# First key stores issued sooner, batch 3's statistics sooner, and turn eight's product order

## The reference

```python
x = x + tanh(g_xattn[0]) * L0_xattn(layernorm(x), ctx, ctx)      # 16 heads, causal
x = x + tanh(g_ffn[0])   * L0_ffn(layernorm(x), w_gate_up, w_proj)   # ternary weights by groups of 64
x = x + tanh(g_xattn[1]) * L1_xattn(layernorm(x), ctx, q_w, ..., o_w)  # q, k normed; softmax over 256 keys
x = x + tanh(g_ffn[1])   * L1_ffn(layernorm(x), w_norm, w_gv, w_out)
# L1_ffn: h = rmsnorm(x) * w_norm; value, gate = quant(h) @ quant(w_gv); u = value * silu(gate)
#         x + quant(u) @ quant(w_out), with 8-bit integers for activations and ternary weights
```

## Time and profile before

| | |
|---|---|
| runs | 1144.2, 1140.21, 1139.71 us, median 1140.21 |
| profiled execution | 1139.14 us, span 1137.4 us |
| PE busy | 1096.0 us of the span |
| DVE, ACT, POOL busy | 832.7, 567.2, 74.5 us |
| mean granted clock of PE | 0.994 |
| transfers | 79.24 MB, most in the first third |

### The profile page before, as it was taken

One profiled execution on the slowest core, in us unless ns is written; L12 is line 12 of the kernel. 1 busy time (PEld: TensorE's weight loads), 2 busy tenths in 40 slices (PEclk: granted clock), 3 DMA queues, 4 the chain that ended last, 5 costly groups with the idle time before them and its releaser, 6 DMA issues.

```text
span 1137.4 us, 25529 instructions
## 1 busy us (share of the span) xinstructions
PE 1096.0 (96%) x10342; PEld 669.3 (59%) x10450; DVE 832.7 (73%) x1440; ACT 567.2 (50%) x918; POOL 74.5 (7%) x180
## 2 busy tenths in 40 slices
PE   8899999999999999999999999899999999999998
PEld 3455555556777777777777655455454545454543
DVE  5688888788767648566565667886868778777795
ACT  3676667766433333333333452455554637372654
POOL 0000000000000000000001012010101010101010
PEclk9899999999999999999999999999999999999999
DMA  9565555443212011021010201101010100000001
GB/s 361 185 194 169 181 193 156 154 122 122 67 38 65 20 38 37 20 75 28 29 57 20 84 2 38 37 2 56 1 57 1 57 1 30 10 11 11 10 10 38
DMA packets 29268, 79.24 MB, mean 70 GB/s; under 512 B 3041, under 2 KB 3297, under 8 KB 28897
## 3 DMA queue, kind: packets, MB, share of 16 engines
q1 hardware_dynamic: 29152, 77.61, 21.0%
HBM read 65.02 MB, written 12.58 MB: 68 GB/s over the span
## 4 chain that ended last, share of the span: by engine, by line
PE 89%; issue 3%; ACT 3%; DVE 2%; DMA 2%; SPq 1%; POOL 0%; ACTq 0%; DVEq 0%; POOLq 0%
PE bank L587 10%; PE bank L586 10%; PE bank L692 10%; PE bank L672 9%; PE bank L545 9%; PE bank L795 8%; PE bank L425 5%; PE bank L825 5%; PE bank L783 5%; PE bank L745 3%; PE bank L764 3%; PE bank L477 2%; PE bank L498 2%; PE bank L510 2%; PE bank L450 2%
## 5 line engine op out<-in xcount | busy, mean ns | idle before, releaser
L586 PE MATMUL bank<-ARENA,W 128*128 128x256 f16 x1024 | 227.3, 273 | 0.7 <-issue 0.7
L587 PE MATMUL bank<-ARENA,W 128*128 128x256 f16 x1024 | 227.2, 273 | 0.0
L1002 ACT ACTIVATE ARENA<-bank 128x512 f32<-128x512 f32 (+3 forms) x143 | 92.9, 687 | 81.3 <-PE bank L425 32.6
L545 PE MATMUL bank<-ARENA 128*128 128x512 f32 x256 | 119.4, 609 | 1.4 <-DMA ARENA<-in_wkv 1.4
L795 PE MATMUL bank<-W,ARENA 128*128 128x512 bf16 x493 | 116.6, 382 | 2.5 <-issue 0.7
L692 PE MATMUL bank<-ARENA 128*128 128x512 f32 x256 | 116.9, 600 | 0.0
L672 PE MATMUL bank<-W,ARENA 128*128 128x512 bf16 x472 | 114.6, 379 | 2.2 <-issue 0.2
L586 PEld LDWEIGHTS bank<-ARENA,W 128*128 128x128 bf16 x1024 | 100.0, 98 | 19.5 <-issue 1.3
L587 PEld LDWEIGHTS bank<-ARENA,W 128*128 128x128 bf16 x1024 | 100.1, 98 | 17.9
L1002 ACT ACTIVATE ARENA<-ARENA 128x512 f16<-128x512 f32 x64 | 40.3, 630 | 136.1 <-DVE ARENA L1585 129.6
L1585 DVE SCALAR_TENSOR_TENSOR ARENA<-bank,ARENA 128x512 f32<-128x512 f32 x64 | 48.0, 750 | 76.4 <-PE bank L587 73.5
(11 more groups left out here) (179 smaller groups left out, 1766.5 us busy)
## 6 DMA issues: line engine op xcount, KB each, us to landing
W<-in_w SPq DMA_DIRECT2D x48, 512.0 KB, 4.0
ARENA<-in_w SPq DMA_DIRECT2D x24, 512.0 KB, 3.6
kv_store<-ARENA SPq DMA_DIRECT2D x32, 256.0 KB, 3.8
W<-kv_store SPq DMA_DIRECT2D x15, 512.0 KB, 4.0
ARENA<-in_ctxT SPq DMA_DIRECT2D x8, 512.0 KB, 3.8
X<-in_x SPq DMA_DIRECT2D x8, 512.0 KB, 5.8
ARENA<-in_ctx SPq DMA_DIRECT2D x8, 512.0 KB, 5.9
out<-X SPq DMA_DIRECT2D x16, 256.0 KB, 2.0
```

Source lines behind the costliest of these rows:

```text
L545: mm = pe.matmul(bank, bufA["KT"][:, b % 2 * KD + k, t * P:(t + 1) * P], W[:, k, :], start=(k == 0), stop=(k == KD - 1 and what == 1))
L586: pe.matmul(bank[:, i * S:(i + 1) * S], W0[:, at:at + P], xt_half(b, 0)[:, k, :], start=(k == 0), stop=False)
L587: mm = pe.matmul(bank[:, i * S:(i + 1) * S], W0[:, at:at + P], xt_half(b, 1)[:, k, :], start=False, stop=(k == KD - 1))
L1002: return act.activation(to, src, ACT.Copy)
```

## The change

On SP the first store of keys is issued behind the constants and ahead of `load_w0(1)`, the second behind `load_values(0)` and ahead of `load_w0(2)`. On DVE, in turn 2, `stats(3)` goes ahead of `d_weighted(0)` and `c_norm_x(3)` ahead of the first `c_weigh`. In the eighth turn PE takes `d_turn_u(d, 0)` and `d_out_product(d, 0)` between the groups of the attention and `d_turn_u(d, 1)` ahead of the last `c_weigh`; ACT rounds both halves of the first tile between gates 5 and 6, and the second tile ahead of the last exponentials; DVE makes the first integers behind gate 6 and the second between `c_weigh` 1 and 2, and stores and takes the peak ahead of the last `c_weigh`. One bank is changed for it, that of `ut0.1`.

```diff
--- before.py
+++ after.py
@@ -261,7 +261,7 @@
         for turn in range(3, NB):
             places.turn(turn, ("g0 v1 g3 pq0 v6 v7 ut0.0 y0 xt0", "v0 po1 v3 g4 v5 g7 tq1 w1 w2 w3", "po0 g2 kt0 v4 pq1 w0 qt1 ut1.1 y1",
                                "g1 v2 kt1 g5 g6 mt tq0 ut0.1 qt0 ut1.0 xt1"))
-        places.turn(NB, ("g0 v1 g3 v5 v7 w1 w3", "v0 po1 v3 g6 g7 ut0.0 y0", "po0 g2 g4 g5 mt w0 ut0.1", "g1 v2 v4 v6 w2"))
+        places.turn(NB, ("g0 v1 g3 v5 v7 w1 w3", "v0 po1 v3 g6 g7 ut0.0 y0", "po0 g2 g4 g5 mt w0", "g1 v2 v4 v6 ut0.1 w2"))
         places.last.update({n: (s.c_ex, 8 * NB) for n in range(4)})
         a, b, c = NB - 3, NB - 2, NB - 1
         ends = ([("po0", c), ("ut1.0", a), ("ut1.1", a), ("po1", c), ("qt0", b), ("qt1", b), ("y1", a)]
@@ -344,8 +344,10 @@
             sp.dma_start(pre["masks"], masks).then_inc(s.ld_sel, 16)
             sp.dma_start(pre["selq"], selq).then_inc(s.ld_sel, 16)
             sp.dma_start(pre["selc"], selc).then_inc(s.ld_sel, 16)
+            store_kv(0, 0)
             load_w0(1)
             load_values(0)
+            store_kv(0, 1)
             load_w0(2)
             load_x(1)
             load_w1(0)
@@ -353,8 +355,6 @@
             load_w1(1)
             load_w0(3)
             load_w0(4)
-            store_kv(0, 0)
-            store_kv(0, 1)
             for turn in range(1, NB + 1):
                 f, b = turn, turn - 1
                 load_w0(3 * turn + 2)
@@ -962,15 +962,18 @@
             d_value_gate(d, 6)
             c_max_turn(b)
             d_value_gate(d, 7)
-            for g in range(NG):
-                c_probs(b, g)
-                if g:
-                    c_weigh(b, g - 1)
+            c_probs(b, 0)
+            c_probs(b, 1)
+            c_weigh(b, 0)
             d_turn_u(d, 0)
+            c_probs(b, 2)
+            c_weigh(b, 1)
+            d_out_product(d, 0)
+            c_probs(b, 3)
+            c_weigh(b, 2)
+            d_turn_u(d, 1)
             c_weigh(b, 3)
-            d_out_product(d, 0)
             c_project_out(b, 0)
-            d_turn_u(d, 1)
             c_project_out(b, 1)
             d_turn_q(c)
             d_out_product(d, 1)
@@ -1305,19 +1308,19 @@
             d_gate(d, 1)
             d_residual(d, 0)
             d_residual(d, 1)
-            for j in range(2, 8):
+            for j in range(2, 6):
                 d_gate(d, j)
+            both(d_round_u, d, 0)
+            d_gate(d, 6)
+            d_gate(d, 7)
             warm(ACT.Exp)
             c_probs(b, 0)
-            d_round_u(d, 0, 0)
             c_probs(b, 1)
-            d_round_u(d, 0, 1)
+            both(d_turn_u, d, 0)
             c_probs(b, 2)
-            d_round_u(d, 1, 0)
+            both(d_round_u, d, 1)
             c_probs(b, 3)
             warm(ACT.Silu)
-            both(d_turn_u, d, 0)
-            d_round_u(d, 1, 1)
             both(d_turn_u, d, 1)
             d_residual(c, 0)
             d_residual(c, 1)
@@ -1875,13 +1878,13 @@
             c_add_out(0, 1)
             v.wait_ge(s.c_xo, 2)
             d_spread(0)
+            stats(3, s.c_ve)
             d_weighted(0)
             d_peak(0)
+            c_norm_x(3)
             c_weigh(1, 0)
             d_inputs(0)
             c_weigh(1, 1)
-            stats(3, s.c_ve)
-            c_norm_x(3)
             c_weigh(1, 2)
             c_weigh(1, 3)
 
@@ -1946,18 +1949,18 @@
             d_value_gate(d, 5)
             c_max_rows(b)
             d_value_gate(d, 6)
+            d_integers16(d, 0)
             d_value_gate(d, 7)
             d_scale_u(d, 1)
+            c_weigh(b, 0)
             d_weighted(c)
-            c_weigh(b, 0)
-            d_integers16(d, 0)
             c_weigh(b, 1)
+            d_integers16(d, 1)
+            c_weigh(b, 2)
+            d_store(d, 0)
             d_peak(c)
-            c_weigh(b, 2)
             c_weigh(b, 3)
             d_inputs(c)
-            d_integers16(d, 1)
-            d_store(d, 0)
             c_add_out(b, 0)
             c_add_out(b, 1)
             v.wait_ge(s.c_xo, 2 * b + 2)
```

## The result

The changed kernel takes 1145.2 us (median of 8 runs, 1144.0 to 1150.6) against 1140.49 (8 runs, 1139.3 to 1144.2): a ratio of 1.0045, 95% interval 1.003 to 1.006, so 4.7 us slower. 1146 was forecast, in a range of 1140 to 1151. The 4.7 us are 0.4%: they lie just under the line of 0.5% (5.7 us) that the prediction drew, so its case "same" (0.41) came about, and not "slower by over 0.5%" (0.52).

What follows compares the result with a forecast made beforehand. TensorE, busy 96% of the span, was taken as the bound. 1139.1 - 1.6 - 0.75 + 6.0 + 2.4 = 1145.2 us against the profiled execution; 1.07 added for the median gave 1146.3, stated as 1146, range 1140 to 1151.

Steps and rivals of the forecast that it cites:

- same: Whole kernel: the outcome that the time stays within 0.5% (5.7 us) of the kernel before; chance 0.41.
- slower by over 0.5%: Whole kernel: the outcome that the time rises by more than 0.5% (5.7 us); chance 0.52.
- Part 1: First stage, moved key stores: third copy sooner, but next batch's weights become the wait; 1.6 us gained.
- Part 2: Turn 2, DVE's statistics and norm sooner: PE then waits for a bank; 0.75 us gained, not 2.8.
- Part 3, first stall: Eighth turn: ACT's roundings wait for the scale, delaying gate 6 and PE's `g7`; 2.5 us lost.
- Second stall: Eighth turn: PE's `c_project_out(b, 0)` waits uncovered for DVE's last `c_weigh`; 3.3 us lost, ends 1.0 to 3.4.
- Clock: Behind the eighth turn's two stalls: stretches of low clock, 1.2 us lost for each, 2.4 together, between 0 and 3.4.
- rival (a): Eighth turn: the clock costs more, both stalls paid in full and a longer stretch behind the first; 1149 to 1152; chance 0.17.
- The row at 719.66: Turn 2, kernel before: the clock stayed full behind PE's 2.8 us wait, taken as evidence against counting both stalls in full.
- (b): Eighth turn: only one stall occurs, costing 2.5 to 3.3 us, with one stretch of low clock; 1141 to 1143; chance 0.17.
- (c): Eighth turn: not slower if the scale is done early and the last `c_weigh` covered; 1133 or 1137; chance 0.11.
- (d): First stage or turn 2 loses: held loads land late, PE goes on at 33 or later; 1149; chance 0.05.

Runs made afterwards that it cites:

- e8: e1 plus, in ACT's first turn, the fourth copy ahead of the signs of piece 3; 1137.26 us, ratio 0.9975 to the kernel before.
- e11: Kernel before with both key stores between `load_w0(3)` and `load_w0(4)`; 1138.9 us, ratio 0.9983.
- e1: Kernel before with only the change's two store moves on SP; 1140.17 us, ratio 0.9997.
- e3: Kernel before with only the eighth turn changed; 1148.88 us, ratio 1.0073.
- e9: e2 plus the second tile of `d_turn_q` in turn 2 in bank 4 instead of bank 5; 1136.55 us, ratio 0.9966 to the kernel before.
- e4: Changed kernel with DVE's `d_scale_u(d, 0)` moved to behind the fourth `d_value_gate`; median 1144.68 us, ratio 1.0033 to the kernel before.
- e6: Changed kernel with DVE's last `c_weigh` ahead of `d_store(d, 0)` and `d_peak(c)`; 1145.93 us, ratio 1.0042 to the kernel before.
- e5: Changed kernel with PE's `d_out_product(d, 1)` between its last `c_weigh` and the two `c_project_out`; 1146.74 us, ratio 1.0049 to the kernel before.
- e2: Kernel before with only DVE's new order in turn 2; 1139.19 us, ratio 0.9983.
- e13: Kernel before with e11's store placing, e8's order (group mean left behind the signs) and e9; eighth turn as before; 1134.67 us, ratio 0.9946.
- e12: Kernel before with e1, e8 with the group mean also ahead of the signs, and e9; eighth turn as before; 1136.08 us, ratio 0.9959.
- e7: Changed kernel with both the scale move of e4 and the product move of e5; 1142.01 us, ratio 1.0008 to the kernel before.

## Why the prediction was right

- *Part 1*, 1.6 us forecast, 0.4 measured alone (its interval reaches to 1.5). That the next batch's piece becomes the wait is shown by ACT's row and by e8 and e11. The mis-sized term is the landing: "everything behind is later by the stores' own 1.3 us" was 2.5 in e1, and 2.3 on the average of the eight profiles with this placing, against the six without. "It does not run dry" held in e1 but not in the changed kernel's profile, which moved 269 GB/s from 18 to 22 us where the kernel before moved 401. The low clock in the profile of e1 lasted 6.8 us for 10.2 before, but that of e3, whose first turn is unchanged, has 6.8 too, so it isn't a gain of the stores.
- *Part 2*, 0.75 us forecast, 1.4 measured by the medians, 1.9 by the ratio (0.7 to 3.1). The steps came out to a tenth: DVE's norm at 710.68 (forecast 710.6), PE's second q tile at 718.66 (718.55). The bank was shown to be the cause of the wait by e9.
- *Part 3, first stall.* `g7` began 3.8 us behind the transpose ahead of it, and the wait was 3.55 us, the scale's place the cause (e4). The net of it, 2.5 us, came out: 3.55 for 0.92 before is 2.6 more, with the 1.28 standing again.
- *Second stall*, 3.3 forecast, 3.14 measured; the small wait for the exponentials, 0.2 forecast, 0.24. Its bounds were wrong at the lower end: without store and peak the stall is 2.3, not 1.0 (e6).
- *Clock*, 2.4 us: e3 gives 8.3 for 6.0 of waits, 2.3 us. That this came out so near is in part luck. The profile of the change paid 5.8 there: behind the first stall the clock was low for 6.8 us, through the small products, and again for 3.4 behind the 1.29, as rival (a) has it. In the median run it was less: the changed kernel's runs list a mean clock of 0.993 at the median, e3's 0.991, those of the kernel before beside e3 0.994, and a thousandth is 1.1 us by the estimate above. Behind each of the two stalls the clock was low in every profile that has it (the first: the changed kernel's, e3, e5, e6; the second: the changed kernel's, e3, e4, e6). But the unchanged turn pays too: the profiles of e1, e2 and e13 have 3.4 us of low clock behind its wait of 1.28, that of e8 has 6.8, those of before, e9, e11 and e12 none. The row at 719.66, which spoke against counting both stalls in full, was one execution: in e1 the same wait of 2.79 us, ended at 718.45, was followed by this:

```profile
719.10:722.50 3.40, 3.40 (x32) 1.67 (x34) 1.75 (x2) 2.68 (x4) 0.00 (x0) 0.50 0.02 5
```

e3 and e11 have it as well. The Trainium skill (TensorE: Matmul & The Clock Gate, Part 1) says that how many products of one kernel run at the low clock varies from run to run. These traces agree: behind the same first stall of 3.5 us the clock was low for 6.8 and 3.4 us in the changed kernel's profile, and for 3.4 in that of e6. It doesn't say that a stall of 3.3 us must be paid, as the prediction has it; that only the rows can show.
- *The sum.* Part 1 gave 1.2 us less than forecast and part 2 some 0.7 more, so that 1146 lies within 1 us of 1145.2 is helped by errors that offset each other. The two stalls, which make the sign, stood where they were forecast and with their lengths.
- *Rivals.* (b) is excluded: both stalls are in each profile of the unmended turn. (c) hung on the scale and on cover for the last division. e4 shows that the scale's place did decide, but with both conditions met (e7) the kernel took 1142.0, not 1137 or 1133: (c) had left out that the product used as cover opens 2.6 us of waits where it stood. (d) happened in small: `load_w0(3)` landed late, and PE went on at 32.0 in e1, not at 33.
- *The order of landing.* Copies and signs found their pieces in order in each profile, so what was missed was how late they land, not their order. It wasn't strict for all transfers: before the change the gates (2 KB, issued at 3.66) landed 6.3 us later, at 10.0, ahead of the constants (128 KB, issued at 3.15), which took 7.1 and landed at 10.2. That agrees with the Trainium skill (DMA: Bandwidth & Descriptors, HWDGE ordering), by which completion isn't first in, first out for an issuing engine; it cost nothing here.

## What to carry to other kernels

An early transfer is worth no more than the time until the next thing in the waiting engine's list is there, not its own lateness. And an issuing list that waits for a result holds up the loads behind it: here a piece that was needed soon landed 2.3 us later. When the order of one stretch is copied to another, look at what each wait had as cover there (here a product between division and projection, and a scale three places sooner), and at whose reader a bank waits for. A product can cover one wait only: moved ahead, it opens the place it came from.

## What was not expected

The two moved stores are 512 KB, 1.3 us at the queue's pace, but the piece behind them landed 1.4 to 3.4 us later than the 26.7 to 27.4 of the kernels without the move (28.8 to 30.1). The extra comes at another transfer in each execution: at the load behind the second store in e1 (2.7 us behind it for 1.3), at `load_w1(1)` in e7 (3.0), and in e12 at none before piece 3, but there the last load ahead of the first store (`selc`) had landed at 17.4 already, for 16.4 before. In e1 the queue had moved as much by 24 us as before (8.47 and 8.48 MB), so there the bytes weren't late, only the landing of single transfers. What makes them late was not followed up.

The clock behind the stalls of the eighth turn was low for 3.4 us in some executions and for 6.8 in others, and one kernel's runs can fall in two groups 5 us apart (e4). The kernel before does this too, on a smaller scale: of its 29 runs beside e1 to e4, 20 took 1138.5 to 1141.4 us at a mean clock of 0.993 to 0.996, and nine took 1142.3 to 1143.8 at 0.991. With such a kernel a single profile says little on the time.
